# One turn of a language-model tower gets an order of its own: the last group's scores between the second MLP products of the group before, its output product in the score banks, its biases and residual behind the gates

## The reference

```
z = (z + d * (Bu - A * y)) / (1 + d * d * A)
y = y + d * z
out = einsum(y, C)
yout = (out + D_skip * u) * silu(zgate)
x = x + yout @ out_proj_w.T + out_proj_b
x = x + gelu(rms(x) @ fc1_w.T + fc1_b) @ fc2_w.T + fc2_b
```

## Time and profile before

| | us |
|---|---|
| median of 3 runs | 1336.01 |
| lowest, highest | 1335.78, 1336.26 |
| profiled execution | 1340.35 |
| its span (first to last instruction) | 1338.0 |
| PE busy | 1130.1 |
| DVE busy | 1078.9 |
| POOL busy | 821.7 |
| ACT busy | 786.6 |

### The profile page before, as it was taken

How to read it: one execution, slowest core, us unless ns; L and a number is a source line. 1 busy time by engine, 2 the same in 40 slices (tenths; PEclk the granted TensorE clock), 3 DMA queues, 4 the chain that set the end, 5 groups by cost and what they waited for, 6 DMA issues and landing times. The chain is left out here.

```text
span 1338.0 us, 24711 instructions
## 1 busy us (share of the span) xinstructions
PE 1130.1 (84%) x7206; PEld 750.8 (56%) x7206; DVE 1078.9 (81%) x1770; ACT 786.6 (59%) x1275; POOL 821.7 (61%) x2278
## 2 busy tenths in 40 slices
PE   3981034589999999999999999999999999997957
PEld 1550012457575757575666666575757566756634
DVE  5988959959797979797978888787979796976078
ACT  4666546374748484747484756656574748452367
POOL 8881020576777878787878777878787877760000
PEclk9999997699999999999999999999999999998879
DMA  9999801010101010101010000000010101000015
GB/s 366 406 409 415 335 11 29 15 35 3 36 2 36 2 36 0 36 2 34 7 30 13 23 18 19 18 19 20 16 31 5 36 1 37 2 18 1 0 59 193
DMA packets 62274, 92.77 MB, mean 69 GB/s; under 512 B 9117, under 2 KB 55026, under 8 KB 57826
## 3 DMA queue, kind: packets, MB, share of 16 engines
q1 hardware_dynamic: 58530, 82.10, 17.2%
q0 software_dynamic: 3072, 8.39, 1.6%
q10 hardware_dynamic: 576, 1.31, 0.3%
HBM read 81.29 MB, written 10.49 MB: 69 GB/s over the span
## 5 line engine op out<-in xcount | busy, mean ns | idle before, releaser
L771 POOL TENSOR_TENSOR stp<-Gs,X 128x32 f32<-128x32 f32 x960 | 289.6, 302 | 182.1 <-ACT X L746 110.4
L773 POOL TENSOR_TENSOR Gs<-Gs,stp 128x32 f32<-128x32 f32 x960 | 283.4, 295 | 75.8
L1151 PE MATMUL bank<-w_fc,gl 128*128 128x256 f32 x1024 | 244.4, 382 | 5.5 <-ACT gl L1142 5.5
L1132 PE MATMUL bank<-mT,w_fc 128*128 128x512 f32 x512 | 240.4, 603 | 1.4 <-ACT mT L1112 1.4
L626 PE MATMUL bank<-xT,w_in 128*128 128x512 f32 x512 | 233.8, 600 | 0.1
L1151 PEld LDWEIGHTS bank<-w_fc,gl 128*128 128x128 f32 x1024 | 189.8, 190 | 69.3 <-issue 31.2
L921 ACT ACTIVATE uT<-bank,cols 128x512 f32<-128x512 f32 x64 | 47.9, 775 | 220.4 <-DVE sz L1055 175.2
L626 PEld LDWEIGHTS bank<-xT,w_in 128*128 128x128 f32 x512 | 93.7, 190 | 99.0 <-issue 93.0
L1132 PEld LDWEIGHTS bank<-mT,w_fc 128*128 128x128 f32 x512 | 96.3, 193 | 88.5 <-issue 82.7
L935 DVE SCALAR_TENSOR_TENSOR uT<-bank,cols,uT 128x500 f32<-128x500 f32 (+1 forms) x192 | 133.4, 733 | 2.7 <-ACT uT L921 0.4
L344 DVE TENSOR_TENSOR peak<-ring,peak 128x1536 f32<-128x1536 f32 (+2 forms) x67 | 115.3, 1721 | 7.8 <-ACT ring L246 6.2
(11 more groups left out here) (198 smaller groups left out, 1845.6 us busy)
## 6 DMA issues: line engine op xcount, KB each, us to landing
ring<-in_table SPq DMA_DIRECT2D x31, 1536.0 KB
d_rep<-d_rows SPq DMA_DIRECT2D x128, 64.0 KB, 2.7
out<-res SPq DMA_DIRECT2D x16, 512.0 KB, 2.9
b_rep<-bc_rows SPq DMA_DIRECT2D x128, 32.0 KB, 1.8
c_rep<-bc_rows SPq DMA_DIRECT2D x128, 32.0 KB, 1.8
w_fc<-in_w_fc SPq DMA_DIRECT2D x2, 1024.0 KB, 8.5
ring<-in_table SPq DMA_DIRECT2D x2, 768.0 KB
w_in<-in_w_in ACTq DMA_DIRECT2D x1, 1088.0 KB
```

What stands on the lines that cost most here:

```text
L771: pool.tensor_tensor(stp[:], Gs[:, t, ::-1, :], X2[:, t, :, :], ALU.mult).then_inc(rec.sem, 1)
L773: pool.tensor_tensor(Gs[:, t + 1, :, :], Gs[:, t, :, :], stp[:], ALU.add).then_inc(rec.sem, 1)
L1132: last = pe.matmul(pj[n % 4][:, :], w_fc1[:, k, n * P:(n + 1) * P], mT[:, k, :], start=(k == 0), stop=(k == KD - 1))
L1151: last = pe.matmul(sbk[j // 2][:, (j % 2) * D:(j % 2 + 1) * D], gl[n % LEAD][:, j * LEN:(j + 1) * LEN], w_fc2[:, n, :], start=False, stop= ...
```

## The change

- PE, turn 16: at n = 8, before fc2 5, come all four transposes and scores 0; at n = 9, before fc2 6, scan_out of half 0 and scores 1; at n = 10, before fc2 7, scan_out of half 1. The output product follows, into tb instead of `sbk`, and without the wait for h2 of the group before.
- ACT, turn 16: utok comes between gelu 6 and gelu 7 instead of behind gelu 7.
- DVE, turn 16: biases of group 15 and h2 of group 14 come behind all gates and ahead of x2; before, they stood between queries 1 and the first skip. x2 reads tb.
- ACT, turns 17 and 18: x3 of group g - 3 comes ahead of the gelus instead of behind them. DVE, turns 17 and 18: max3 of that group comes ahead of h2 instead of behind it.
- All other turns keep their order (`last` is true in turn 16 alone, `fourth and not second` in turns 17 and 18 alone).

```diff
--- before.py
+++ after.py
@@ -1054,23 +1054,23 @@
                 dve.wait_ge(z_ready.sem, z_ready.at(g))
                 dve.tensor_tensor(sz[:, f, :], sz[:, f, :], uT[:, f, :], ALU.mult).then_inc(yg_ready.sem, 1)
 
-        def pe_out(pe, g):
+        def pe_out(pe, g, bank):
             pe.wait_ge(m_ready.sem, m_ready.at(g))
-            if since(g):
+            if since(g) and bank is sbk:
                 pe.wait_ge(h2_ready.sem, h2_ready.at(g - 1))
             for n in range(2):
                 for j in (2 * n, 2 * n + 1):
                     for f in range(UT):
                         if j == 0:
                             pe.wait_ge(yg_ready.sem, yg_ready.at(g, f + 1))
-                        last = pe.matmul(sbk[n][:, (j % 2) * D:(j % 2 + 1) * D], sz[:, f, j * LEN:(j + 1) * LEN],
+                        last = pe.matmul(bank[n][:, (j % 2) * D:(j % 2 + 1) * D], sz[:, f, j * LEN:(j + 1) * LEN],
                                          w_out[:, f, :], start=(f == 0), stop=(f == UT - 1))
                 last.then_inc(o_mm.sem, 1)
 
-        def dve_x2(dve, g, n):
+        def dve_x2(dve, g, n, bank):
             dve.wait_ge(biased.sem, biased.at(g, 1))
             dve.wait_ge(o_mm.sem, o_mm.at(g, n + 1))
-            dve.tensor_tensor(xl[:, 2 * n:2 * n + 2, :], sbk[n][:, :].rearrange("p (j c) -> p j c", j=2),
+            dve.tensor_tensor(xl[:, 2 * n:2 * n + 2, :], bank[n][:, :].rearrange("p (j c) -> p j c", j=2),
                               xl[:, 2 * n:2 * n + 2, :], ALU.add).then_inc(x2_ready.sem, 1)
 
         def act_sum_squares(act, g, n):
@@ -1229,6 +1229,7 @@
         def pe_turn(pe):
             def turn(g, first, second, third, fourth, nxt):
                 p, m = g - 1, g - 2
+                last = second and not first
                 for f in range(UT):
                     if first and f == 2:
                         pe_transpose_rows(pe, g)
@@ -1243,31 +1244,42 @@
                 for n in range(FT + LEAD):
                     if third and n < FT:
                         pe_fc1(pe, m, n, p if second else None)
-                    if second and n == FT:
+                    if last and n == FT:
+                        for j in range(G):
+                            pe_u_T(pe, p, None, j)
+                        pe_scores(pe, p, 0)
+                    if last and n == FT + 1:
+                        pe_scan_out(pe, p, 0, 0)
+                        pe_scan_out(pe, p, 0, 1)
+                        pe_scores(pe, p, 1)
+                    if last and n == FT + 2:
+                        pe_scan_out(pe, p, 1, 0)
+                        pe_scan_out(pe, p, 1, 1)
+                    if second and first and n == FT:
                         pe_u_T(pe, p, g if first else None, 0)
                         pe_u_T(pe, p, g if first else None, 1)
-                    if second and n == FT + 1:
+                    if second and first and n == FT + 1:
                         pe_u_T(pe, p, g if first else None, 2)
                         pe_u_T(pe, p, g if first else None, 3)
-                    if second and n == FT + 2:
+                    if second and first and n == FT + 2:
                         pe_scores(pe, p, 0)
                     if third and n >= LEAD:
                         pe_fc2(pe, m, n - LEAD)
                     if first and n == 1:
                         pe_ss(pe, g)
-                if second:
+                if second and first:
                     pe_scan_out(pe, p, 0, 0)
                     pe_scan_out(pe, p, 0, 1)
                     pe_scores(pe, p, 1)
                 if first and second:
                     pe_u(pe, g, (0, 1))
-                if second:
+                if second and first:
                     pe_scan_out(pe, p, 1, 0)
                     pe_scan_out(pe, p, 1, 1)
                 if first:
                     pe_u(pe, g, (2, 3))
                 if second:
-                    pe_out(pe, p)
+                    pe_out(pe, p, sbk if first else tb)
             turns(pe, turn)
 
         def act_turn(act):
@@ -1304,7 +1316,11 @@
                     act_small_rsqrt(act, g)
                     if not second:
                         act_u_tap0(act, g, (2, 3))
+                if fourth and not second:
+                    act_x3(act, g - 3, GROUPS - 1)
                 for n in range(FT):
+                    if second and not first and n == FT - 1:
+                        act_utok(act, p)
                     if third:
                         act_gelu(act, m, n)
                     if second and n == 0:
@@ -1315,10 +1331,10 @@
                         act_rep(act, g, (1,))
                     if second and n == 5:
                         act_layer_norm(act, p)
-                if second:
+                if second and first:
                     act_utok(act, p)
-                if fourth:
-                    act_x3(act, g - 3, p if second else GROUPS - 1)
+                if fourth and second:
+                    act_x3(act, g - 3, p)
                 if first and second:
                     act_u_tap0(act, g)
                 if nxt:
@@ -1369,8 +1385,11 @@
                         dve_mask(dve, p, 0, hh)
                 if second and not (first and third):
                     dve_queries(dve, p, 1)
+                if second and first and not third:
                     dve_biases(dve, p)
-                if third:
+                if fourth and not second:
+                    dve_max3(dve, g - 3)
+                if third and (first or not second):
                     dve_h2(dve, m)
                 if second:
                     dve_skip(dve, p, (0, 1))
@@ -1379,18 +1398,21 @@
                     dve_gate(dve, p, (0, 1))
                     dve_skip(dve, p, (2, 3))
                     dve_gate(dve, p, (2, 3))
+                if second and not first:
+                    dve_biases(dve, p)
+                    dve_h2(dve, m)
                 if first and second:
                     dve_conv_u(dve, g, (0, 1))
                     dve_conv_u(dve, g, (2,))
                 if second:
-                    dve_x2(dve, p, 0)
+                    dve_x2(dve, p, 0, sbk if first else tb)
                 if first and second:
                     dve_conv_u(dve, g, (3,))
                 if second:
-                    dve_x2(dve, p, 1)
+                    dve_x2(dve, p, 1, sbk if first else tb)
                 if first and second:
                     dve_bc(dve, g)
-                if fourth:
+                if fourth and second:
                     dve_max3(dve, g - 3)
                 if third:
                     for j in range(G):
```

## The result

| | before | changed |
|---|---|---|
| median, lowest, highest of 9 runs each, us | 1335.92, 1333.80, 1337.25 | 1332.93, 1330.04, 1336.06 |
| ratio of the runs, 95% interval | | 0.9980, 0.9971 to 0.9990 |
| profiled execution, its span | 1340.35, 1338.0 | 1332.93, 1330.6 |

What follows compares the result with a forecast made beforehand. Turn 16 was taken as bound by TensorE, VectorE, TensorE again, then the chain from x2 to rows; turn 17 by VectorE's end. Gains 4.92 + 1.32 = 6.2 us; 1336.01 - 6.2 = 1329.8, range 1327.0 to 1333.0.

Steps and rivals of the forecast that it cites:

- the first of turn 16: Transposes and copies, TensorE, turn 16: scores 0 start 1.69 us earlier, at the price of 0.23 and 1.25 us standing.
- Rival A: Turn 16: the clock falls at the new short gaps, costing 1.5 to 3.8 us; gain 2.4 to 4.7, time 1332.5; chance 0.10.
- The rest of the sum: Turn 16: masks 1 start 4.0 us earlier, the 4.36 us wait goes, biases and h2 hide under the output; turn gains 4.92.
- The tail: End of turn 17, VectorE: max3 of group 14 leaves the chain behind h2, gaining 1.32 us.
- The clock in turn 17: The 4.90 us gap before the MLP transposes stays, and its clock fall still costs 3.8 us, possibly as little as 1.5.
- B: Turn 17: the clock comes back earlier, up to 3.8 us more gain, time about 1327.9 with half of it; chance 0.10.
- C: Turn 16: masks 1 come late for another reason, the gap only moves; gain only 3.0 us, time 1333.0; chance 0.06.
- D: Turn 16: the low clock lasts until the output, up to 13.5 us more work, time 1343; chance 0.04.
- the step from it to the median: Whole run: the 4.3 us between profiled execution and median lies outside the turns changed, so 6.2 comes off 1336.01.

Runs made afterwards that it cites:

- 1: Changed kernel plus three 256-column matmuls, result unused, between the last transposition and scores 0 of turn 16; ratio 0.9937 to the kernel before.
- 5: Kernel before with only turn 16's four transpositions together, utok ahead of gelu 7 and scores 0 ahead of fc2 5; ratio 1.0011 to the kernel before.
- 4: Changed kernel with the fc2 products of turn 16 spread over TensorE's stops, partly in halves, and gelu 7 ahead of utok again; ratio 0.9947 to the kernel before.
- 10: The same kernel as 4, run again beside a quieter kernel before and for a second trace; ratio 0.9949 to the kernel before.
- experiment 2: Kernel before with only the moves in turns 17 and 18, x3 ahead of the gelus and max3 ahead of h2; ratio 0.9973 to the kernel before.
- 3: Kernel before with only VectorE's part and the other bank in turn 16: biases and h2 behind the gates, output into tb; ratio 0.9959 to the kernel before.
- 6: Kernel 4 plus five 512-column matmuls, result unused, between turn 16's output and the next MLP transpositions; 1325.6 us, ratio 0.9926 to the kernel before.
- 7: Kernel 6 plus nine unused matmuls behind the last fc2 of turn 17 and three ahead of the third stage's first transposes; ratio 0.9944 to the kernel before.
- kernel 9: Kernel before, nothing moved, plus five 512-column matmuls, result unused, between turn 16's output and turn 17's MLP transpositions; ratio 0.9972 to the kernel before.

## Why the prediction was wrong

- **The step that failed** is the first of turn 16: "This costs TensorE 0.23 and 1.25 us of standing that it did not have, the price of this step". The stops came, 0.33 and 1.50 long. Their price was 0.35 us more of standing than worked out and, beyond it, a fall of the clock worth 3.3 us in one execution and 1.6 in the other, a term that the sum put at nothing. It was shown three ways: filling the stop takes it away (1), making the stop in the kernel before brings it (5), and spreading the work takes it away with no filler (4, 10).
- **Rival A was what happened**, with a chance of 0.10 against 0.70. Its price was right: gain 2.4 to 4.7 forecast, 2.5 (27.84, with 1.33 of tail) and 4.2 (26.20) by the traces, 2.7 timed. The weighing was wrong. The prediction called the trace silent between stops of 0.74 and 3.32 us, and I read that silence as safety. It was not silent on either side:

```profile
606.16 1.09 PE L1105 MATMUL bank<-ident,xr 128*128 128x128 f32 x8 [1.07 <-ACT xr L1099]
```

```profile
600.00:614.00 14.00, 12.57 (x72) 6.62 (x71) 8.96 (x25) 10.89 (x26) 11.30 (x37) 1.00 0.15 42
...
1217.44:1219.50 2.06, 0.00 (x1) 0.00 (x0) 2.06 (x4) 0.00 (x0) 0.00 (x0) 1.00 0.00 0
1219.50:1226.30 6.80, 4.50 (x34) 4.08 (x35) 5.56 (x10) 0.00 (x0) 0.00 (x0) 0.50 0.00 0
```

  Three stops of 1.07 and 1.08 us in the steady turns left the clock full. And in the stop of 4.36 us the clock was down after 2.06 us of standing, as the mean of 0.74 also says: that fall had not needed 3.3. The section "A second HAM failure mode: psum-queue depth-cycling" of the Trainium skill's page "TensorE: Matmul & The Clock Gate", by which short idle spells between groups of matmuls make the clock swing between its two levels, had spoken for rival A; the traces agree with it in direction, with falls behind 1.47 to 2.01 us in four executions of four.
- **The rest of the sum held.** Masks 1 waited for scores 1 and no longer for biases and h2; scan_out and output ran without a wait; biases and h2 hid under the output (x2 0 began right behind h2, at 1225.15, by an estimate from half of the output's 7.07 us 0.4 late, and x2 1 began 0.1 us behind the output). With the stop filled S1 was 24.57 for 24.13, and 0.38 of the 0.44 is the later start of the scores (3.99 us behind the first transposition for 3.61).
- **The tail** gave its 1.33 for 1.32.
- **The clock in turn 17** cost what was said and scattered as said: S2 lies between 36.3 and 37.9 in the nine traces that leave its gap open.
- **Rivals B, C and D** did not come. B has no more than 0.8 us of S2 in the first trace of the changed kernel, against it 0.4 the other way in the second, and experiment 2, with the order of before in turn 16, has 1.1: that is scatter. D needed 12.4 us at half speed; the longest in turn 16 was 6.8. Its argument took the longest low stretch of before for 8.5 us; with the part inside the gap it was 10.2 (1236.6 to 1246.8), so D stood on less than it seemed.
- The profiled execution of before was 4.3 us above its median. The transposition mark, 3.9 us later than in the changed kernel, points to where: ahead of turn 16. As far as that shows, the step from it to the median was sound.

## What to carry to other kernels

Before moving work on TensorE, list the stops that the new order makes, and count each one of 1.5 us or more as a possible fall of the clock, with several microseconds of half speed behind it, even where the trace at hand has falls behind longer ones alone; an order that shortens the longest stop but makes a new one of 1.5 us can lose most of its gain. Look through the whole trace for stops of the same length, not only the turn at hand. Spread independent products over all the stops in pieces small enough to fit, and fill what is left with matmuls whose result nobody reads. Compare stretches between marks inside the program when the total scatters by more than the effect.

## What the runs showed of the hardware

- Stops of TensorE of 1.47, 1.50 and 2.01 us, in a stream that was otherwise busy, were followed by half clock (2.4 to 1.2 GHz) for 3.4 to 6.8 us in four executions of four (changed kernel twice, 3, 5). The engine was busy again when the clock fell, for 0.5 to 1.8 us: at 1205.3 in the changed kernel, 0.8 us after the scores had started. Those of 1.47 and 1.50 us had one of 0.33 shortly ahead of them; those of 2.01 had not.
- Stops of 0.95 us (4, 6, 7, 10), of 1.07 and 1.08 us (before) and two of 1.27 us in steady turns of kernel 9 were not followed by a fall.
- The length of one stop does not decide alone. At one place, ahead of the MLP transpositions of turn 2, 2.26 us in kernel 7 came with a fall, and 2.60 us in kernels 1 and 3 came with none:

```profile
285.83 1.09 PE L1105 MATMUL bank<-ident,xr 128*128 128x128 f32 x8 [2.60 <-ACT xr L1099]
```

```profile
283.23:292.00 8.77, 5.82 (x50) 3.47 (x51) 2.87 (x5) 7.88 (x18) 7.21 (x22) 1.00 0.14 38
```

  What else decides, no run here isolates.
- The same stop in the same program cost 1.6 us in one execution and 3.3 in another.
- Matmuls whose results nobody reads kept the clock up at both places: three of 256 columns in the stop of 1.5 us, five of 512 in the gap of 4.9.
